# Two attention layers in one kernel: one set of theta and phi copies, reciprocals a slot sooner

## The chip, the core and the metric

The kernel runs on one core of a Trainium2 chip (trn2). The time is the device time of one execution of the whole program in microseconds, and the median over several executions counts. The core has a matrix engine (TensorE, PE in the profile; its weight loads are PEld), a vector engine (VectorE, DVE), a scalar engine (ScalarE, ACT), GpSimd (POOL) and SyncE (SP). SP computes nothing here: it issues every DMA, one after the other in a fixed order, and a wait in its program holds back all that stands behind it.

## What is computed

32 images of 128 channels by 1024 pixels pass through a non-local block and then an attention block with group norm. All inputs and outputs are float32.

```python
# layer 0, d = 64; t and p are (n, 64, 1024), g is x as (n, 128, 1024)
theta = W_theta x + b_theta;  phi = W_phi x + b_phi
f = softmax(einsum('ndq,ndk->nqk', t, p) / sqrt(64), axis=-1)
x1 = x + W_fuse einsum('nqk,nck->ncq', f, g) + b_fuse
# layer 1, c = 128
h = group_norm(x1, 32 groups, eps=1e-5) * gn_w + gn_b
q, k, v = W_q h + b_q, W_k h + b_k, W_v h + b_v
attn = softmax(einsum('bic,bcj->bij', q, k) / sqrt(128), axis=-1)
y = x1 + W_p einsum('bcj,bij->bci', v, attn) + b_p
```

## The kernel before

**Rounds and slots.** The program is a software pipeline. Each round has 16 slots. In slots 0 to 7 PE makes the scores of the eight 128-query tiles of layer 0 of one image, in slots 8 to 15 those of layer 1 of the image before it, each tile 128 x 1024 in PSUM (`s_ps`, three parts). Every engine has a `body` that goes through the 16 slots and calls its steps; the order of these calls is the order of its instructions. `before(what, it, s)` only counts how often something has happened, to give a semaphore's value. A round takes some 57 us. I write round 992 for the one whose first scores start at 991.83 us of the span, round 934 for 934.24, and round 1049 for 1048.64.

**A tile's way.** PE makes the scores; DVE takes the negated row maximum (L750); ACT takes the exponential (L649) and its float16 part (L674), DVE the rest (L767). Both parts lie in `pair`, and a DMA transpose (L364, issued by SP) turns them into `et`. I call the transpose of the tile of slot t "T" and t. Four tiles are a group. Its last tile (slots 3, 7, 11, 15) is turned by PE instead, and DVE finishes it with L761. Its first one (0, 4, 8, 12) is "copied": its rest is made by POOL (L892, `pair<-e_copied,pair`) in the slots of `LO_SLOTS`, and SP issues its transpose in the slot after that.

**Values.** Six slots after a group's first tile, PE begins its products with the values (`values`, `o_ps<-et,v_hi`), for which all transposes of the group must have landed. So the group of slots 12 to 15 is waited for in slot 2 of the next round, the group of slots 0 to 3 in slot 6.

**Reciprocals.** The row sums `den` of a group become factors on DVE (L779, L784) six slots after its first tile, in slots 6, 10, 14 and 2. SP writes them to DRAM (L378) in the same slot and reads them back onto all partitions (L389) in the slot after; the second of these waits on SP until the first has landed. DVE uses them in `normalised` (L804), ten slots after the group's first tile.

**Theta and phi.** In units `tp0` (slot 10) and `tp1` (slot 12) PE makes theta and phi of the next image, 512 pixels each. ACT stages them (L616), and POOL splits each in the next slot into a high and a low part in `tp_hl0` and `tp_hl1`, theta on partitions 0 to 63, phi on 64 to 127 (L889, L892). Four SBUF-to-SBUF DMAs of each half (L424 to L427) then fill `phi2` and `theta2`, in slot 12 and in slot 14. PE's first scores of a round wait for all eight (L463 to L465).

Of the kernel before, what the change touches and what calls it, by code (L numbers as in the profile page):

```python
# [7 lines left out]
F32 = mybir.dt.float32  # L8
# [6 lines left out]
C = 128  # L15
D = 64
# [7 lines left out]
PV_LAG = 6  # L24
OUT_LAG = 10
Y_LAG = 2

# [3 lines left out]
COPIED = 0  # L31
LO_SLOTS = {0: 2, 4: 7, 8: 10, 12: 14}

PART = (0, 1, 0, 2, 1, 0, 1, 2) * 2
# [23 lines left out]
XS_SLOT = 1  # L58
X_MAX_SLOT = 7
X_SLOT = 8  # L60
X_LO_SLOTS = (9, 11)
H_SLOT = 2
H_LO_SLOTS = (3, 4)
RES_SLOTS = (5, 12)
TP_COPY_SLOTS = {12: "tp0", 14: "tp1"}
TP_COPIES = 4
# [10 lines left out]
def attention_pair(nc: bass.Bass, x, w_theta_t, w_phi_t, w_fuse_t, q_w_t, k_w_t, p_w_t, v_w, vectors,  # L77
# [69 lines left out]
    def before(what, it, s):  # L147

        return value(lambda i: count(what, i, s), it)

    def here(what, it, s):
        return bool(what(SLOTS * it.like + s))
# [48 lines left out]
    with ExitStack() as ctx:  # L201
        def sb(name, shape, dt=F32):
            return ctx.enter_context(nc.sbuf_tensor(name, shape, dt))
# [4 lines left out]
        def sem(name):  # L208
            return ctx.enter_context(nc.semaphore(name))
# [25 lines left out]

        tp_hl = [sb(f"tp_hl{n}", [C, 2, HALF], F32R) for n in range(2)]
        q_hi, q_lo = sb("q_hi", [C, N], F32R), sb("q_lo", [C, N], F32R)
# [74 lines left out]
        s_den = sem("den_scaled_ready")  # L312
        s_tp_copy = [sem(f"theta_phi_copied{n}") for n in range(2)]
        s_split_hi = sem("unit_split_hi")
# [24 lines left out]
        def _(sp):  # L339
# [9 lines left out]
            def transposes(it, s):  # L349
                if here(crossed_at, it, s - 2):  # L350
                    move(it, s - 2, crossed_at, s_pair)
                for t in [t for t in LO_SLOTS if LO_SLOTS[t] == s - 1]:
                    move(it, t, copied_at, s_copied)
# [14 lines left out]
            def reciprocals_out(it, s):  # L368
                first = s - 6
                if not (first % GROUP == 0 and here(tile_at, it, first)):  # L370
                    return
                n, g = before(group_at, it, first), first // GROUP % 2
                sp.wait_ge(s_rden, n + 1)
                sp.sem_inc(s_carrier)

                sp.wait_ge(s_rden_row[g], 16 * before(same_group(first), it, first))
                sp.sem_inc(s_carrier)
                sp.dma_start(rden_dram[g], rden[:, g, :]).then_inc(s_rden_dram[g], 16)  # L378

            def reciprocals_in(it, s):  # L380
                first = s - 7
                if not (first % GROUP == 0 and here(tile_at, it, first)):
                    return
                n, g = before(group_at, it, first), first // GROUP % 2
                sp.wait_ge(s_rden_dram[g], 16 * before(same_group(first), it, first) + 16)
                sp.sem_inc(s_carrier)
                sp.wait_ge(s_taken, or_none(n - 1))
                sp.sem_inc(s_carrier)
                sp.dma_start(rden_row[:, g, :],  # L389
                             rden_dram[g].rearrange("q t -> (q t)").partition_broadcast(P)).then_inc(s_rden_row[g], 16)  # L390
# [21 lines left out]
            def tp_copies(it, s):  # L412
                unit = next((u for u, name in UNITS.items() if name == TP_COPY_SLOTS.get(s)), None)
                if unit is None or not here(tp_at, it, unit):
                    return
                half = int(UNITS[unit][-1])
                cols = slice(half * HALF, (half + 1) * HALF)
                sp.wait_ge(s_split, before(staged_at, it, unit) + 1)
                sp.sem_inc(s_carrier)

                sp.wait_ge(s_scores, before(tile_at, it, PHASE))
                sp.sem_inc(s_carrier)
                theta_hl, phi_hl = (tp_hl[half][rows, :, :].bitcast(F32) for rows in (slice(0, D), slice(D, C)))
                sp.dma_start(phi2[0:D, :, cols].bitcast(F32), phi_hl).then_inc(s_tp_copy[half], 16)  # L424
                sp.dma_start(phi2[D:C, :, cols].bitcast(F32), phi_hl).then_inc(s_tp_copy[half], 16)  # L425
                sp.dma_start(theta2[0:D, cols].bitcast(F32), theta_hl[:, 0, :]).then_inc(s_tp_copy[half], 16)  # L426
                sp.dma_start(theta2[D:C, cols].bitcast(F32), theta_hl[:, 1, :]).then_inc(s_tp_copy[half], 16)  # L427

# [14 lines left out]
        def _(pe):  # L443
# [7 lines left out]
            def scores(it, s, half):  # L451
                if not here(tile_at, it, s):
                    return
                if half == 0:
# [8 lines left out]
                    if s == 0:  # L463
                        for n in range(2):
                            pe.wait_ge(s_tp_copy[n], 16 * TP_COPIES * before(mx_at, it, 0))  # L465
                    if s == PHASE:
# [233 lines left out]
        def _(dve):  # L700
# [70 lines left out]
            def reciprocals(it, s):  # L771
                first = s - 6
                if not (first % GROUP == 0 and here(tile_at, it, first)):
# [104 lines left out]
        def _(pool):  # L878
# [15 lines left out]
            def split_units(it, s):  # L894
# [7 lines left out]
                if name[0] == "t":  # L902

                    pool.wait_ge(s_tp_copy[half], 16 * TP_COPIES * or_none(before(mx_at, it, s) - 1))
                    hi, lo = tp_hl[half][:, 0, :], tp_hl[half][:, 1, :]
                    hi_read = hi.bitcast(F32)
# [150 lines left out]
```

## Time and profile before

| | us |
|---|---|
| median of 3 runs | 1922.38 (1917.98 to 1924.8) |
| the profiled execution | 1909.72 |
| its span in the trace | 1907.9 |
| PE busy in it | 1715.2 (90%) |
| POOL, ACT, DVE busy | 1381.1, 1409.7, 1359.3 |

The profile is one execution, 0.66% below the median of the runs. Its times are from the start of the span. The chain that ended last is made up of PE to 44%, of SP's queue to 20%, of "issue" to 12% and of DMAs to 8%. The issuing time of a DMA on SP and the time until it lands are two things: a row of SP's queue shows the first, and the page lists medians of the second: 3.8 us for the theta copies, 4.6 us for the transposes, 2.1 us for the reciprocals' write. The page's DMA share is the mean over 16 engines.

### The profile page before, as it was taken

Reading aid. Unit: us, or ns where it says so; the run is one execution under the profiler, and the core shown is the slowest. Engines: PE = TensorE matmul, PEld = TensorE weight load, DVE = VectorE, ACT = ScalarE, POOL = GpSimd, SP = SyncE. Lnnn points to the kernel's source line nnn. Section 1 sums busy time; section 2 is a strip of 40 time slices with the busy share of each in tenths; the row PEclk is TensorE's granted clock in tenths of the full one; section 3 lists DMA queues with packets and bytes.
Section 4 is the critical chain, followed back from the end, with each engine's and each line's share of the span. In section 5 each row is a group of like instructions: output and inputs, shape, how many; then the busy total and the mean of one; then the engine's idle time right before and its main releaser. Section 6 shows DMA issues by size and latency. Waiting matters only on the chain.

```text
span 1907.9 us, 34651 instructions
## 1 busy us (share of the span) xinstructions
PE 1715.2 (90%) x8970; PEld 1127.0 (59%) x8970; DVE 1359.3 (71%) x1541; ACT 1409.7 (74%) x2088; POOL 1381.1 (72%) x1449
## 2 busy tenths in 40 slices
PE   4698989999999999999989999999999999999986
PEld 3465655665656665665655655665656666655653
DVE  4577777777777777777777777777777777777764
ACT  3577777778777777877777877777877777877764
POOL 3567776778777778777778777678777778877754
PEclk9999999999999999999999999999999999999999
DMA  4688888888888888888887878888878988878874
GB/s 94 127 160 169 165 174 166 182 178 171 171 176 180 178 181 167 170 170 177 180 182 166 172 169 181 174 175 172 173 170 172 187 180 168 170 168 184 167 145 94
DMA packets 879542, 319.90 MB, mean 168 GB/s; under 512 B 825376, under 2 KB 826272, under 8 KB 879520
## 3 DMA queue, kind: packets, MB, share of 16 engines
q1 hardware_dynamic: 879520, 319.65, 81.3%
q8 instruction: 9, 0.15, 0.0%
q14 instruction: 13, 0.11, 0.0%
HBM read 50.86 MB, written 17.04 MB: 36 GB/s over the span
## 4 chain that ended last, share of the span: by engine, by line
PE 44%; SPq 20%; issue 12%; DMA 8%; POOL 5%; ACT 5%; DVE 4%; POOLq 0%; ACTq 0%; DVEq 0%
PE o_ps L448 17%; PE s_ps L448 16%; SPq L364 10%; PE m_ps L448 6%; DMA theta<-tp_hl 6%; PE s_ps L487 5%; SPq L426 2%; SPq L424 2%; SPq L427 2%; SPq L425 2%; DVE neg_max L750 2%; DMA rden_dram<-rden 1%; POOL k_lo L892 1%; DVE pair L767 1%; ACT e L649 1%
## 5 line engine op out<-in xcount | busy, mean ns | idle before, releaser
L750 DVE TENSOR_REDUCE neg_max<-s_ps 128x1 f32<-128x1024 f32 x512 | 625.5, 1222 | 233.3 <-PE s_ps L448 232.7
L448 PE MATMUL o_ps<-et,v_hi 128*128 128x512 f16 x2048 | 702.7, 385 | 57.5 <-issue 31.2
L448 PE MATMUL s_ps<-phi,theta 128*128 128x512 f32 x1024 | 334.5, 450 | 95.2 <-DMA theta<-tp_hl 86.2
L448 PE MATMUL o_ps<-et,v_lo 128*128 128x512 f16 x1024 | 393.4, 384 | 0.0
L448 PEld LDWEIGHTS o_ps<-et,v_hi 128*128 128x128 f16 x2048 | 204.8, 100 | 303.0 <-issue 98.2
L767 DVE SCALAR_TENSOR_TENSOR pair<-s_ps,pair 128x1024 f16<-128x1024 f32 x256 | 311.2, 1216 | 16.8 <-ACT pair L674 16.8
L649 ACT ACTIVATE s_ps<-s_ps,neg_max 128x1024 f32<-128x1024 f32 x256 | 277.3, 1083 | 58.9 <-DVE neg_max L750 58.3
L448 PEld LDWEIGHTS s_ps<-phi,theta 128*128 128x128 f32 x1024 | 197.2, 196 | 167.6 <-issue 102.4
L892 POOL TENSOR_TENSOR pair<-e_copied,pair 128x1024 f16<-128x1024 f32 x128 | 273.8, 2139 | 22.5 <-ACT pair L672 22.5
L761 DVE SCALAR_TENSOR_TENSOR et<-s_ps,et 128x1024 f16<-128x1024 f32 x128 | 156.8, 1225 | 175.4 <-ACT et L659 175.4
L674 ACT ACTIVATE pair<-s_ps 128x1024 f16<-128x1024 f32 x256 | 261.9, 1023 | 17.5
L448 PE MATMUL s_ps<-k_hi,q_hi 128*128 128x512 f32 x512 | 249.4, 487 | 4.4 <-POOL q_lo L892 2.1
L448 PE MATMUL s_ps<-k_hi,q_lo 128*128 128x512 f32 x512 | 202.0, 395 | 0.0
L448 PE MATMUL s_ps<-k_lo,q_hi 128*128 128x512 f32 x512 | 200.5, 392 | 0.0
L649 ACT ACTIVATE e<-s_ps,neg_max 128x1024 f32<-128x1024 f32 x128 | 142.6, 1114 | 52.5 <-DVE neg_max L750 52.4
L659 ACT ACTIVATE et<-s_ps 128x1024 f16<-128x1024 f32 x128 | 131.1, 1024 | 62.5 <-PE s_ps L487 55.7
L986 POOL TENSOR_TENSOR x<-x,xr 128x512 f32<-128x512 f32 x64 | 81.6, 1275 | 110.1 <-DVE x L804 110.0
L487 PE MATMUL s_ps<-ident_sb,e 128*128 128x128 f32 x1024 | 147.8, 292 | 10.4 <-ACT e L649 10.3
L892 POOL TENSOR_TENSOR v_lo<-stage,v_hi 128x512 f16<-128x512 f32 x128 | 148.2, 1157 | 10.7
L487 PEld LDWEIGHTS s_ps<-ident_sb,e 128*128 128x128 f32 x1024 | 129.2, 153 | 34.8 <-ACT e L649 23.3
L649 ACT ACTIVATE e_copied<-s_ps,neg_shifted 128x1024 f32<-128x1024 f32 x128 | 142.9, 1116 | 4.1
L448 PEld LDWEIGHTS o_ps<-et,v_lo 128*128 128x128 f16 x1024 | 101.8, 99 | 69.4 <-issue 3.3
(130 smaller groups left out, 2873.0 us busy)
## 6 DMA issues: line engine op xcount, KB each, us to landing
phi<-tp_hl SPq DMA_DIRECT2D x128, 256.0 KB, 3.8
rden_row<-rden_dram SPq DMA_DIRECT2D x128, 256.0 KB, 3.8
xs<-in_x SPq DMA_DIRECT2D x32, 512.0 KB, 4.0
theta<-tp_hl SPq DMA_DIRECT2D x128, 128.0 KB, 3.8
out_y<-y_sb SPq DMA_DIRECT2D x64, 256.0 KB, 2.4
et<-pair SPq DMA_TRANSPOSE x384, 4.6
rden_dram<-rden SPq DMA_DIRECT2D x128, 2.0 KB, 2.1
w_f<-in_w_fuse_t SPq DMA_DIRECT2D x1, 64.0 KB, 2.3
```

The lines of the kernel that those rows point to most:

```text
L364: sp.dma_start_transpose(et[:, t // GROUP % 4, r, :, :], pair[:, place(t), :, :].rearrange("q a n -> q (a n)")).then_inc(s_pair_t[place(t) ...
L424: sp.dma_start(phi2[0:D, :, cols].bitcast(F32), phi_hl).then_inc(s_tp_copy[half], 16)
L448: mm = pe.matmul(out, lhs_t, rhs, start=start and n == 0, stop=stop and n == len(terms) - 1)
L487: mm = pe.transpose(s_ps[:, part(t), kb * P:(kb + 1) * P], e[:, kb * P:(kb + 1) * P], ident[:, :])
L649: nc.scalar.activation(to[:, :], s_ps[:, r, :], ACT.Exp, bias=bias, accum_out=den[:, g, t % GROUP:t % GROUP + 1]).then_inc(s_exp, 1)
L659: nc.scalar.activation(et[:, t // GROUP % 4, TURNED, 0:KB, :], s_ps[:, part(t), :].rearrange("k (b q) -> k b q", b=KB), ACT.Copy, scale=E_ ...
L674: nc.scalar.activation(pair[:, r, 0, :], s_ps[:, part(t), :], ACT.Copy, scale=E_SCALE).then_inc(s_pair_hi, 1)
L750: nc.vector.tensor_reduce(neg_max[:, t % 4:t % 4 + 1], s_ps[:, part(t), :], AX.X, ALU.max, negate=True).then_inc(s_max, 1)
L761: nc.vector.scalar_tensor_tensor(out=blocks[:, KB:2 * KB, :], in0=s_ps[:, part(t), :].rearrange("k (b q) -> k b q", b=KB), scalar=E_SCALE, ...
L767: nc.vector.scalar_tensor_tensor(out=pair[:, r, 1, :], in0=s_ps[:, part(t), :], scalar=E_SCALE, in1=pair[:, r, 0, :], op0=ALU.mult, op1=AL ...
L892: nc.gpsimd.tensor_tensor(out, in_, hi, ALU.subtract).then_inc(sem, 1)
L986: nc.gpsimd.tensor_tensor(x1[:, cols], x1[:, cols], xr[:, cols], ALU.add).then_inc(s_x1, 1)
```

## The change

It does three things.

- **One set of copies.** `tp_hl0` and `tp_hl1` become one tile `tp_hl` of 1024 columns. SP issues four DMAs of twice the size, all in slot 13, after it has waited for the split of `tp1`. They replace four in slot 12 and four in slot 14; the diff shows one of the four. One semaphore replaces two.
- **Reciprocals a slot sooner.** With `REC_LAG = 5` DVE makes them in slots 5, 9, 13 and 1; SP writes them in the same slots and reads them back in slots 6, 10, 14 and 2. In slot 13 the write stands ahead of the copies, in slot 1 ahead of the image load.
- **The last copied tile first.** T12 is issued in slot 14, ahead of T13, and no longer in slot 15 behind it.

```diff
+REC_LAG = 5
+COPIED_OUT_SLOTS = {0: 3, 4: 8, 8: 11, 12: 14}
-TP_COPY_SLOTS = {12: "tp0", 14: "tp1"}
+TP_COPY_SLOT = 13
...
-        tp_hl = [sb(f"tp_hl{n}", [C, 2, HALF], F32R) for n in range(2)]
+        tp_hl = sb("tp_hl", [C, 2, N], F32R)
...
             def transposes(it, s):
                 if here(crossed_at, it, s - 2):
                     move(it, s - 2, crossed_at, s_pair)
-                for t in [t for t in LO_SLOTS if LO_SLOTS[t] == s - 1]:
+                for t in [t for t in COPIED_OUT_SLOTS if COPIED_OUT_SLOTS[t] == s]:
                     move(it, t, copied_at, s_copied)
...
             def reciprocals_out(it, s):
-                first = s - 6
+                first = s - REC_LAG
...
             def reciprocals_in(it, s):
-                first = s - 7
+                first = s - REC_LAG - 1
...
             def tp_copies(it, s):
-                unit = next((u for u, name in UNITS.items() if name == TP_COPY_SLOTS.get(s)), None)
-                if unit is None or not here(tp_at, it, unit):
-                    return
-                half = int(UNITS[unit][-1])
-                cols = slice(half * HALF, (half + 1) * HALF)
-                sp.wait_ge(s_split, before(staged_at, it, unit) + 1)
+                if s != TP_COPY_SLOT or not here(mx_at, it, MX_SLOT):
+                    return
+                sp.wait_ge(s_split, before(staged_at, it, s))
...
-                sp.dma_start(phi2[0:D, :, cols].bitcast(F32), phi_hl).then_inc(s_tp_copy[half], 16)
+                sp.dma_start(phi2[0:D, :, :].bitcast(F32), phi_hl).then_inc(s_tp_copy, 16)
...
             def reciprocals(it, s):
-                first = s - 6
+                first = s - REC_LAG
```

On SP, in the repeated round, from slot 11 on. Before (L364 are the transposes, here T9, T8, T10, then T13 and T12 behind the copies):

```order
L364 DMA_TRANSPOSE et<-pair 128x16x128
L418 ISA
L421 ISA
L424 DMA phi2<-tp_hl0 64x2x512
L425 DMA phi2<-tp_hl0 64x2x512
L426 DMA theta2<-tp_hl0 64x512
L427 DMA theta2<-tp_hl0 64x512
L376 ISA
L378 DMA rden_dram<-rden 128x4
L418 REGISTER_ALU
L424 DMA phi2<-tp_hl1 64x2x512
L425 DMA phi2<-tp_hl1 64x2x512
```

The same place after the change (the line numbers are four to five higher):

```order
L368 DMA_TRANSPOSE et<-pair 128x16x128
L380 ISA
L382 DMA rden_dram<-rden 128x4
L419 ISA
L422 ISA
L425 DMA phi2<-tp_hl 64x2048
L426 DMA phi2<-tp_hl 64x2048
L427 DMA theta2<-tp_hl 64x1024
L428 DMA theta2<-tp_hl 64x1024
L389 REGISTER_ALU
L393 DMA rden_row<-rden_dram 128x512
```

The reciprocals' write moved from between the two sets to ahead of the single one; eight copies became four.

On DVE, around slot 1, before and after as one piece of the difference. The first row is the last operation on the turned tile of slot 15:

```order
 L761 SCALAR_TENSOR_TENSOR et<-s_ps,et 128x1024
+L779 SCALAR_TENSOR_TENSOR den_scaled<-den,v_scale1,e_factors 128x4
+L783 ISA
+L784 RECIPROCAL rden<-den_scaled 128x4
 L749 REGISTER_ALU
 L750 TENSOR_REDUCE neg_max<-s_ps 128x1
 L793 REGISTER_ALU
-L794 ISA
-L804 TENSOR_TENSOR y_sb<-o_ps,rden_row 128x512
-L779 SCALAR_TENSOR_TENSOR den_scaled<-den,v_scale1,e_factors 128x4
-L784 RECIPROCAL rden<-den_scaled 128x4
```

The two small operations moved ahead of a row maximum and of `normalised`.

## Rows read from the trace of the kernel before

**Rows 1.** The page: busy time and its share of the span, by engine.
```profile
PE 1715.2 (90%) x8970; PEld 1127.0 (59%) x8970; DVE 1359.3 (71%) x1541; ACT 1409.7 (74%) x2088; POOL 1381.1 (72%) x1449
```

**Rows 2.** Waits of PE: total us, times, longest; other waits left out.
```profile
PE s_ps L448 <- DMA theta<-tp_hl: 86.2, 31, 5.0
PE o_ps L448 <- issue: 31.2, 33, 2.4
PE o_ps L448 <- POOL k_lo L892: 15.2, 12, 1.5
...
PE o_ps L448 <- DMA et<-pair: 11.0, 6, 3.6
```

**Rows 3.** PE in time: start, us, line; brackets: idle before, releaser.
```profile
991.83 1.17 PE L448 MATMUL s_ps<-phi,theta 128*128 128x512 f32 x4 [2.50 <-DMA theta<-tp_hl]
...
1013.88 0.38 PE L448 MATMUL o_ps<-et,v_hi 128*128 128x512 f16 x1 [1.13 <-POOL k_lo L892]
```

**Rows 4.** The chain that ended last, in the round starting at 934.24: start, us.
```profile
942.28 4.12 DMA rden_dram<-rden
...
947.25 2.97 SPq L364
...
952.69 4.52 DMA et<-pair
```

**Rows 5.** SP's queue in time: transposes, copies, reciprocals (start, us of issuing).
```profile
973.51 7.82 SPq L364 DMA_TRANSPOSE et<-pair  x3
981.68 0.67 SPq L424 DMA_DIRECT2D phi<-tp_hl  x1
...
985.47 0.37 SPq L378 DMA_DIRECT2D rden_dram<-rden  x1
986.10 0.62 SPq L424 DMA_DIRECT2D phi<-tp_hl  x1
...
988.13 1.29 SPq L427 DMA_DIRECT2D theta<-tp_hl  x1
...
990.31 7.76 SPq L364 DMA_TRANSPOSE et<-pair  x3
...
1003.51 7.82 SPq L364 DMA_TRANSPOSE et<-pair  x3
...
1060.28 8.73 SPq L364 DMA_TRANSPOSE et<-pair  x3
```

**Rows 6.** Stretches of the copies: busy by engine, PEclk, DMA share, GB/s.
```profile
984.00:986.00 2.00, 2.00 (x17) 1.58 (x16) 1.97 (x3) 1.47 (x2) 2.00 (x2) 1.00 0.97 188
986.50:987.50 1.00, 1.00 (x6) 0.83 (x5) 0.81 (x2) 0.97 (x3) 1.00 (x2) 1.00 0.39 76
990.00:991.50 1.50, 0.00 (x0) 0.00 (x0) 0.42 (x1) 0.61 (x2) 0.00 (x0) 1.00 0.79 250
```

**Rows 7.** DVE and POOL in time: start, us, instruction.
```profile
979.77 1.23 DVE L761 SCALAR_TENSOR_TENSOR et<-s_ps,et 128x1024 f16<-128x1024 f32 x1 [1.40 <-ACT et L659]
980.16 1.29 POOL L892 TENSOR_TENSOR tp_hl<-stage,tp_hl 128x512 fp32r<-128x512 f32 x1
...
998.90 0.22 DVE L779 SCALAR_TENSOR_TENSOR den_scaled<-den,v_scale,e_factors 128x4 f32<-128x4 f32 x1
...
1000.39 1.21 DVE L767 SCALAR_TENSOR_TENSOR pair<-s_ps,pair 128x1024 f16<-128x1024 f32 x1
...
1058.80 1.21 DVE L767 SCALAR_TENSOR_TENSOR pair<-s_ps,pair 128x1024 f16<-128x1024 f32 x1
```

**Rows 8.** Stretches: two rounds' first parts, then two round starts.
```profile
991.83:1013.88 22.05, 20.00 (x105) 12.95 (x106) 15.61 (x17) 18.36 (x28) 15.80 (x20) 1.00 0.90 195
1048.64:1071.15 22.51, 21.68 (x105) 14.25 (x106) 15.24 (x17) 17.77 (x27) 15.23 (x20) 0.92 0.95 193
...
130.70:132.70 2.00, 2.00 (x9) 1.71 (x9) 0.79 (x1) 0.17 (x1) 0.24 (x2) 0.50 1.25 170
1792.70:1794.70 2.00, 2.00 (x10) 1.76 (x9) 0.95 (x1) 0.17 (x1) 0.41 (x3) 0.53 1.17 201
```

More of the change, by code:

```diff
@@ L312, in attention_pair @@
         s_den = sem("den_scaled_ready")
-        s_tp_copy = [sem(f"theta_phi_copied{n}") for n in range(2)]
+        s_tp_copy = sem("theta_phi_copied")
         s_split_hi = sem("unit_split_hi")
@@ L422, in tp_copies @@
                 sp.sem_inc(s_carrier)
-                theta_hl, phi_hl = (tp_hl[half][rows, :, :].bitcast(F32) for rows in (slice(0, D), slice(D, C)))
-                sp.dma_start(phi2[0:D, :, cols].bitcast(F32), phi_hl).then_inc(s_tp_copy[half], 16)
-                sp.dma_start(phi2[D:C, :, cols].bitcast(F32), phi_hl).then_inc(s_tp_copy[half], 16)
-                sp.dma_start(theta2[0:D, cols].bitcast(F32), theta_hl[:, 0, :]).then_inc(s_tp_copy[half], 16)
-                sp.dma_start(theta2[D:C, cols].bitcast(F32), theta_hl[:, 1, :]).then_inc(s_tp_copy[half], 16)
+                theta_hl, phi_hl = (tp_hl[rows, :, :].bitcast(F32) for rows in (slice(0, D), slice(D, C)))
+                sp.dma_start(phi2[0:D, :, :].bitcast(F32), phi_hl).then_inc(s_tp_copy, 16)
+                sp.dma_start(phi2[D:C, :, :].bitcast(F32), phi_hl).then_inc(s_tp_copy, 16)
+                sp.dma_start(theta2[0:D, :].bitcast(F32), theta_hl[:, 0, :]).then_inc(s_tp_copy, 16)
+                sp.dma_start(theta2[D:C, :].bitcast(F32), theta_hl[:, 1, :]).then_inc(s_tp_copy, 16)
             def body(it):
@@ L463, in scores @@
                     if s == 0:
-                        for n in range(2):
-                            pe.wait_ge(s_tp_copy[n], 16 * TP_COPIES * before(mx_at, it, 0))
+                        pe.wait_ge(s_tp_copy, 16 * TP_COPIES * before(mx_at, it, 0))
                     if s == PHASE:
@@ L902, in split_units @@
                 if name[0] == "t":
-                    pool.wait_ge(s_tp_copy[half], 16 * TP_COPIES * or_none(before(mx_at, it, s) - 1))
-                    hi, lo = tp_hl[half][:, 0, :], tp_hl[half][:, 1, :]
+                    pool.wait_ge(s_tp_copy, 16 * TP_COPIES * or_none(before(mx_at, it, s) - 1))
+                    hi, lo = (tp_hl[:, n, half * HALF:(half + 1) * HALF] for n in range(2))
                     hi_read = hi.bitcast(F32)
```

1 line of the change is left out of this document (added).

## The prediction

> **What bounds the kernel now.** I read the busy shares first, then PE's waits, then one round in time on PE and on SP, then the stretches in which DMAs move.
>
> PE is busy for 90% of the span; no other engine is over 74% [rows 1]. So PE is the bound, and what can be won is its waits. Two kinds make up most of them [rows 2]. Before the first scores of a round PE waits for the theta copies: 86.2 us in 31 rounds, 2.8 each. Before products with the values it waits 31.2 + 15.2 + 11.0 = 57.4 us under three names. The names mislead. In round 934 the chain goes from the landing of the reciprocals' write (942.28 + 4.12 = 946.40) over T1 at 947.25 to T2 at 952.69, which lands at 957.21 and lets PE's products go [rows 4]. So there the wait is for the last transpose of the group, also where the waits name POOL or "issue"; and T1 stood behind the reciprocals on SP.
>
> In round 992 the three waits are 2.50 us before the first scores [rows 3], and between these and the products of slot 6 22.05 - 20.00 = 2.05 us of idle PE [rows 8]: 1.13 in slot 6 [rows 3], the other 0.92 in slot 2, where T14 is the last transpose to be waited for. Two kinds of rounds must be kept apart. In round 992 PE's granted clock is 1.00 throughout (2.4 GHz). In round 1049 it is 0.92 over the same part, PE is busy for 21.68 us with the same 105 matmuls and idle for 0.83 [rows 8]: after the wait for theta it starts at half speed (1.2 GHz). Of the 30 rounds from 130 to 1792 us, 17 start so, the first and the last among them [rows 8], and 13 at full speed. In a half-speed round the slow start uses up what would otherwise be waited.
>
> **Part 1, one set of copies.** Now: T10 is issued by 973.51 + 7.82 = 981.33, the first copy at 981.68, the second set at 986.10, its last at 988.13 [rows 5], and PE starts at 991.83 [rows 3], 10.15 after the first copy. PE could have started 2.50 sooner. Afterwards the first copy waits for three things: T10 (981.33), the split of tp1 (980.16 + 1.29 = 981.45), and the new reciprocals' write ahead of it. The latter needs DVE's L761 (979.77 + 1.23 = 981.00 [rows 7]) and two small operations of some 0.2 us (0.22 for the larger one [rows 7]), so about 981.5. The three come within 0.2 us of each other. The write with what follows it takes 986.10 - 985.47 = 0.63 [rows 5]. The first copy goes out at about 982.35, 0.65 later than now.
>
> Against it stands a hole that goes away. Between the two sets DMA is mostly idle: 986.5 to 987.5 moves at a share of 0.39, so 0.6 us are lost [rows 6]. 0.65 and 0.6 cancel. What is left is the moving itself. The copies of a round are 4 x 256 + 4 x 128 KB = 1.57 MB. With 2.1 us (the time to land of the small reciprocals' write) as the fixed part, they take 10.15 - 2.1 - 0.6 = 7.45 us, 211 GB/s; the DMA engines are busy to 0.97 at 188 GB/s in the middle and 0.79 at 250 at the end [rows 6]. This is a transfer at its limit, and halving the number of DMAs halves neither bytes nor time. Bounds: at 250 GB/s 6.3 us, 1.15 us sooner; at 188 GB/s all the way 8.4 us, 0.95 later. I take 0.2 us sooner, near the middle rate since the same bytes take the same way, a little for fewer and longer rows: 30 x 0.2 = 6 us.
>
> The Trainium skill says otherwise twice (DMA: Bandwidth & Descriptors). "Rules for kernel authors" asks for large transfers, and the fit in "Anatomy of one DMA" (2.0 us and bytes over 436 GB/s, for another issuing path) would give 5.6 us for all 1.57 MB, an estimate. "Why small descriptors are slow (HBM only)" says that SBUF-to-SBUF transfers don't suffer from small ones, which would leave nothing to win. The trace agrees with the second: 188 GB/s at a share of 0.97. By the first the wait for theta would be gone (below, with rival B).
>
> Once there is a loss. At the start of the pipeline tp1's split comes long after tp0's, and nothing but the spacing of the two sets bounds what is lost: 986.10 - 981.68 = 4.4 us at most [rows 5]. I take 3 us.
>
> **Part 2, reciprocals sooner and T12 first.** In round 992 the half of T1 in `pair` is ready at 1000.39 + 1.21 = 1001.60 [rows 7], but SP issues it at 1003.51 [rows 5], since it stands in the wait for the reciprocals' write, whose turn came late and which queued behind transposes and the image load. DVE's two operations begin at 998.90 now; a slot sooner they stand two large operations earlier, of some 1.2 us each [rows 7]. So the write is issued some 2.4 us sooner, ahead of the image load, and the read is out of the way by about 1001. T1 then goes at 1001.8, 1.7 sooner, and T0 and T2 with it, each ready by then. Against this, DVE's two operations now stand ahead of the row maximum of slot 2: 0.45 us, of which its later slack takes half, so 0.25. Net 1.45, and PE's products of slot 6 come at 22.05 - 1.45 = 20.6 after the first scores instead of 22.05. For this the wait in slot 2 (0.92) must shrink too, or 20.00 + 0.92 = 20.9 would be the end. It does in part: with four DMAs less and T12 ahead, SP begins the last three transposes at some 987.5 and not at 990.31 [rows 5]. But DMA is taken by the copies until about 991, so T14 lands only some 0.5 sooner. 20.4 is then under 20.6. For the 13 full-speed rounds I take 1.5: 20 us.
>
> In a half-speed round this gives little. In round 1049 T1 is issued at 1060.28 [rows 5] with its pair ready at 1058.80 + 1.21 = 1060.01 [rows 7]: SP was not late, and at most the 0.83 us of idle PE could go. Other such rounds had T1 held back by a few tenths. Bounds 0 and 0.83; I take 0.4: 17 x 0.4 = 7 us.
>
> The other places to which reciprocals move cost nothing: the writes of slots 5 and 9 fall where SP waits for the next pair anyway (T9 at 973.51 began a new batch). In slot 13 DVE's 0.45 us fall into a wait for PE of about that length. `rden_row` is needed five slots after it is read. If such cover were gone, it would be 0.4 us for each group.
>
> **Sum.** 6 + 20 + 7 - 3 = 30 us. The profiled execution would go from 1909.7 to about 1880; the median of the runs is 0.66% above it now, so from 1922.4 to 1892, 1.6% faster. With the bounds of part 2 and rates near the middle this case runs from 1878 to 1908.
>
> **Rivals.**
>
> A, the gain is only partial: SP is free in time, but something else holds the slot 6 products (T0 or T2 late, or the wait in slot 2 unchanged at 0.92). Then 13 x 0.5 + 6 - 3 = 10 us: 1912. For it: T14 depends on a DMA that is full. Against: the three rows from T1 to T2 follow each other without a gap.
>
> B, the large copies are quicker, and the clock holds. For it: 250 GB/s is seen at the end of the set [rows 6]. Copies 1.15 us sooner leave 1.35 of the 2.50 us wait; a shorter wait might leave the clock at its upper level, and a half-speed round would be like a full one (22.51 to 20.6, 1.5 more than the 0.4 counted). 30 x 1.15 + 17 x 1.5 + 24 = 84 us: 1838. By the Trainium skill's fit named above (DMA: Bandwidth & Descriptors, "Anatomy of one DMA") the wait for theta would end altogether, and the time would be about 1795, an estimate. Against both: the share of 0.97.
>
> C, slower: issuing and landing grow with the size of a DMA, so that merging wins nothing and the set no longer starts early. Now the last copy is issued 2.03 us after the first of its set, and PE goes on 3.70 after that. If both grew by 40%, PE would start at 982.35 + 2.8 + 5.2 = 990.3, sooner than now; doubled, at 982.35 + 4.1 + 7.4 = 993.8, 2.0 us later. The case decides against the change from 24 / 30 = 0.8 us later on, since part 2 gives 24 us. At 1.4 us later: 42 - 24 = 18 us slower, 1940. For it: the gate now has three things that end together, and each delay hits all the bytes. Against: the first set's rate shows that its issues weren't the limit.
>
> D, nothing: what is won before slot 6 is waited for again at the next theta copies, or half-speed starts become more frequent (13 full rounds that turn half-speed lose what they won). 1920.
>
> **Chances.** Forecast 0.50, A 0.10, B 0.17, C 0.12, D 0.11. A measurement of this kernel can tell about 0.3% (6 us) from no change. Faster by more than that: 0.50 + 0.10 + 0.17, and a little of D, 0.78; within it 0.10; slower 0.12. The range takes in the forecast, A, about half of B and most of D: 1840 to 1922. The likeliest time is 1892.
>
> **What the profile will show.** If part 1 is right, PE's wait for theta stays near 2.3 us a round (75 us in all or a little less), with the last copy landing some 10 us after T10's issue, and no hole in the DMA share. If part 2 is right, T1 follows its pair by 0.3 us in all rounds, SP's wait for the reciprocals' write (L386 before) shrinks to under half, and the waits before products fall from 57 to some 25 us. The count of half-speed round starts tells the clock's part. A wait for theta under 1.5 us is B, one over 3.3 us is C. The forecast is wrong if the copies' rate changes by over 10%, or if the number of half-speed starts moves by more than five.

## The result, and the profile after

The changed kernel takes 1907.78 us (median of 5 runs, 1903.28 to 1910.44) beside 1922.38 us before (5 runs, 1917.98 to 1924.8). The ratio is 0.9927, with a 95% interval of 0.9906 to 0.9948: 0.7% or 14.6 us faster, where 30 us were forecast. In a second measurement, beside other runs of the kernel before, the same kernel gave 0.9973 (0.9955 to 0.9991). Both intervals lie below 1, so the gain is real, but it is 0.3 to 0.7%. The larger figure rests on the first measurement alone: there the kernel before took 1922 us, in three later groups 1908 to 1910, and why is not known.

The two profiled executions don't even show it: 1909.72 us before and 1910.44 after. That of before lay 12.7 us under the median of its runs, that of after 2.7 over. The kernel before took such a time in the later groups too. The two still show well what moved, and on what its size depends.

First the page: busy time by engine, then the engines' shares of the chain of work that ended last.

```profile
PE 1738.8 (91%) x8970; PEld 1141.4 (60%) x8970; DVE 1383.4 (72%) x1541; ACT 1404.0 (74%) x2088; POOL 1379.7 (72%) x1449
...
PE 42%; issue 14%; DMA 11%; POOL 11%; ACT 9%; SPq 6%; DVE 4%; POOLq 0%; ACTq 0%; DVEq 0%
```

PE does the same 8970 matmuls as before and is busy for 23.6 us longer [rows 1]. DVE has its 1541 instructions again, and is busy for 24.1 us longer. Both matter below. PE's waits (total us, times, longest):

```profile
PE s_ps L449 <- DMA theta<-tp_hl: 99.7, 31, 8.7
...
PE o_ps L449 <- issue: 10.8, 11, 2.7
...
PE o_ps L449 <- DMA et<-pair: 5.1, 2, 3.3
...
PE o_ps L449 <- DVE y_sb L804: 3.3, 6, 1.2
```

Before products PE waits 20.1 us under all names (k_lo's 0.9 with them), where it was 57.4 [rows 2]: 37 us less. For theta it waits 99.7 instead of 86.2: 13.5 more. All in all its waits are 23 us shorter, and its busy time 23.6 us longer. The busy time is the clock's: stretches of 2 us, each from 0.5 us after a round's first scores on (busy by engine PE, PEld, DVE, ACT, POOL, then the granted clock, DMA share and GB/s):

```profile
1053.60:1055.60 2.00, 2.00 (x15) 1.63 (x15) 1.23 (x1) 0.32 (x2) 0.71 (x3) 1.00 1.14 219
1109.64:1111.64 2.00, 2.00 (x9) 1.71 (x8) 0.60 (x1) 0.17 (x1) 0.13 (x1) 0.50 1.07 219
```

Of the 30 rounds behind the start-up, 5 start at full clock like the first row, 25 wholly or partly at half like the second; before it was 13 and 17 [rows 8]. I sorted the rounds by the clock of this stretch, and took the mean time from one round's first scores to the next's:

| | rounds, full clock | their mean, us | rounds, mostly at half | their mean, us | third round begins at |
|---|---|---|---|---|---|
| before | 13 | 57.07 | 10 | 57.51 | 130.2 |
| after | 5 | 56.26 | 17 | 57.45 | 135.4 |
| after, second measurement | 9 | 56.22 | 13 | 57.26 | 137.0 |

(The rest have a clock between 0.6 and 0.98 in it, and the last has no successor.) So full-speed rounds became 0.8 us shorter, half-speed rounds did not, and full-speed rounds became rare. The second measurement's profiled execution had 9 of them and a span 9 us shorter. That goes with the lower median of the changed kernel there, 1901.79 us instead of 1907.78. Why its lead was nevertheless smaller it doesn't explain: that comes from the kernel before, which took 1909.95 us instead of 1922.38.

### The profile page after: what moved, and what is told of

Same layout as the page of the kernel before. It is cut to its first block, busy times and chain, and to the rows that moved or that the text cites. A ratio compares the mean times of both kernels' runs of the same rounds, so it can differ in the third digit from the quotient of the medians.

```text
span 1908.6 us, 34400 instructions
## 1 busy us (share of the span) xinstructions
PE 1738.8 (91%) x8970; PEld 1141.4 (60%) x8970; DVE 1383.4 (72%) x1541; ACT 1404.0 (74%) x2088; POOL 1379.7 (72%) x1449
## 4 chain that ended last, share of the span: by engine, by line
PE 42%; issue 14%; DMA 11%; POOL 11%; ACT 9%; SPq 6%; DVE 4%; POOLq 0%; ACTq 0%; DVEq 0%
PE o_ps L449 15%; PE s_ps L449 15%; DMA theta<-tp_hl 10%; PE m_ps L449 6%; PE s_ps L487 6%; SPq L427 3%; ACT s_ps L649 3%; POOL x_lo L892 2%; ACT et L659 2%; DVE den_scaled L779 2%; ACT h_hi L628 2%; ACT e L649 2%; DVE neg_max L750 1%; POOL tp_hl L892 1%; POOL y_sb L996 1%
## 5 line engine op out<-in xcount | busy, mean ns | idle before, releaser
L449 PE MATMUL o_ps<-et,v_hi 128*128 128x512 f16 x2048 | 709.9, 388 | 20.5 <-issue 10.8
L449 PE MATMUL s_ps<-phi,theta 128*128 128x512 f32 x1024 | 343.3, 460 | 108.9 <-DMA theta<-tp_hl 99.7
L449 PEld LDWEIGHTS s_ps<-phi,theta 128*128 128x128 f32 x1024 | 201.8, 201 | 184.1 <-DMA theta<-tp_hl 102.6
L892 POOL TENSOR_TENSOR pair<-e_copied,pair 128x1024 f16<-128x1024 f32 x128 | 274.2, 2142 | 22.2 <-ACT pair L672 22.2
L761 DVE SCALAR_TENSOR_TENSOR et<-s_ps,et 128x1024 f16<-128x1024 f32 x128 | 156.8, 1225 | 180.0 <-ACT et L659 180.0
L674 ACT ACTIVATE pair<-s_ps 128x1024 f16<-128x1024 f32 x256 | 262.2, 1024 | 17.6
L659 ACT ACTIVATE et<-s_ps 128x1024 f16<-128x1024 f32 x128 | 131.1, 1024 | 71.8 <-PE s_ps L487 65.4
L487 PE MATMUL s_ps<-ident_sb,e 128*128 128x128 f32 x1024 | 155.0, 301 | 12.1 <-ACT e L649 12.1
L487 PEld LDWEIGHTS s_ps<-ident_sb,e 128*128 128x128 f32 x1024 | 135.5, 159 | 37.9 <-ACT e L649 27.0
L892 POOL TENSOR_TENSOR v_lo<-stage,v_hi 128x512 f16<-128x512 f32 x128 | 148.2, 1158 | 10.7
L672 ACT ACTIVATE pair<-e_copied 128x1024 f16<-128x1024 f32 x128 | 135.3, 1057 | 9.2
```

The lines of the kernel that those rows point to most:

```text
L449: mm = pe.matmul(out, lhs_t, rhs, start=start and n == 0, stop=stop and n == len(terms) - 1)
L487: mm = pe.transpose(s_ps[:, part(t), kb * P:(kb + 1) * P], e[:, kb * P:(kb + 1) * P], ident[:, :])
L659: nc.scalar.activation(et[:, t // GROUP % 4, TURNED, 0:KB, :], s_ps[:, part(t), :].rearrange("k (b q) -> k b q", b=KB), ACT.Copy, scale=E_ ...
L672: nc.scalar.activation(pair[:, r, 0, :], e_copied[:, :], ACT.Copy).then_inc(s_copied_hi, 1)
L674: nc.scalar.activation(pair[:, r, 0, :], s_ps[:, part(t), :], ACT.Copy, scale=E_SCALE).then_inc(s_pair_hi, 1)
L761: nc.vector.scalar_tensor_tensor(out=blocks[:, KB:2 * KB, :], in0=s_ps[:, part(t), :].rearrange("k (b q) -> k b q", b=KB), scalar=E_SCALE, ...
```

## What stands ahead of the copies

This is one round of the changed kernel in time: DVE, then POOL, SP and PE (start, us, instruction; in brackets the idle time before and what ended it).

```profile
1040.14 1.23 DVE L761 SCALAR_TENSOR_TENSOR et<-s_ps,et 128x1024 f16<-128x1024 f32 x1 [1.40 <-ACT et L659]
1041.28 1.13 DVE L779 SCALAR_TENSOR_TENSOR den_scaled<-den,v_scale,e_factors 128x4 f32<-128x4 f32 x1
1042.54 0.18 DVE L784 RECIPROCAL rden<-den_scaled 128x4 f32<-128x4 f32 x1
```

```profile
1041.11 1.29 POOL L892 TENSOR_TENSOR tp_hl<-stage,tp_hl 128x512 fp32r<-128x512 f32 x1
```

```profile
1033.65 7.08 SPq L368 DMA_TRANSPOSE et<-pair  x3
1042.98 0.33 SPq L382 DMA_DIRECT2D rden_dram<-rden  x1
1043.65 0.51 SPq L425 DMA_DIRECT2D phi<-tp_hl  x1
...
1046.77 2.50 SPq L428 DMA_DIRECT2D theta<-tp_hl  x1
1049.53 1.08 SPq L393 DMA_DIRECT2D rden_row<-rden_dram  x1
1050.86 8.55 SPq L368 DMA_TRANSPOSE et<-pair  x3
```

```profile
1053.10 1.19 PE L449 MATMUL s_ps<-phi,theta 128*128 128x512 f32 x4 [3.37 <-DMA theta<-tp_hl]
1062.14 0.39 PE L449 MATMUL o_ps<-et,v_hi 128*128 128x512 f16 x1 [0.94 <-issue]
1074.53 0.38 PE L449 MATMUL o_ps<-et,v_hi 128*128 128x512 f16 x1 [0.45 <-DVE y_sb L804]
```

Three things are to be seen.

- **SP stands idle for over 2 us.** T9, T8 and T10 are out at 1033.65 + 7.08 = 1040.73, not 7.82 but 7.08 after they began [rows 5]. The first copy leaves at 1043.65. T10 is no gate any more; all the copies wait for the split of the last half and for the reciprocals' write.
- **A 4-column operation takes 1.13 us.** The sums' scaling, L779, takes 0.21 alone. Here it overlaps POOL's L892, which runs till 1042.39, and ends at 1042.41, 0.02 behind it. The write follows, and behind it the copies. Over the whole execution the scaling takes over 0.3 us in 71 of 128 cases, before in 25, and each of the 71 ends within 0.03 us behind the end of an instruction of POOL; together it takes 74.9 us instead of 49.4, which is all the growth of DVE's busy time. In 14 of the 30 rounds the first copy left some 1.25 us after the split, in 14 others 0.24, in two between.
- **The issues grew.** From the first copy to the last it is 3.12 us where a set took 2.03 before, and PE starts 6.33 after the last, where it was 3.70.

The Trainium skill has the second point (SBUF — State Buffer, "Who interferes with whom"): a DVE instruction with two inputs from SBUF contends with a GpSimd instruction that reads SBUF, and whichever engine has the shared pair keeps it for a whole instruction. The trace agrees: 1.13 us instead of 0.21, and the end 0.02 us behind POOL's. The reciprocal behind it, with one input, took 0.18 in all 128 cases, also in the 57 that lay inside an instruction of POOL with two inputs.

## Experiments

The kernels ran in three groups of four, each with the kernel before beside it, at 1908.15, 1908.53 and 1909.95 us. That is 0.7% under the 1922.38 of the first measurement, so ratios are compared, not times. The same changed kernel gave 0.9927 in one group and 0.9973 in another, so between groups a difference of half a per cent tells nothing.

### The reciprocals alone

```diff
 (kernel before)
+REC_LAG = 5
-                first = s - 6
+                first = s - REC_LAG
...
-                first = s - 7
+                first = s - REC_LAG - 1
```

> Only the reciprocals move a slot sooner; two sets of copies in slots 12 and 14 as before. My theory (the single set starts too late, since it waits for the split of tp1 and for a reciprocals' write that POOL holds up): the waits before products fall as they did after the change (from 57 to about 20 us), and the first set of copies can start right behind T10, which is now issued sooner; the wait for theta falls from 86 to about 60 us. Time 1855 to 1885, clearly below the changed kernel's 1908. The rival (merging the copies is good, and what went wrong is only that more rounds start at half speed): no better than the changed kernel, 1903 to 1915.

Measured: 1973.86 us, ratio 1.0352 (1.0323 to 1.0380), 3.5% slower. Both expectations were wrong. SP in one round says why:

```profile
1071.00 0.68 SPq L425 DMA_DIRECT2D phi<-tp_hl  x1
...
1073.23 1.28 SPq L428 DMA_DIRECT2D theta<-tp_hl  x1
1074.79 0.36 SPq L379 DMA_DIRECT2D rden_dram<-rden  x1
1077.20 0.33 SPq L390 DMA_DIRECT2D rden_row<-rden_dram  x1
1077.78 0.62 SPq L425 DMA_DIRECT2D phi<-tp_hl  x1
```

The write now stands in slot 13, and the read in slot 14 ahead of the second set of copies. SP issues in order, and the read must wait until the write has landed: from 1075.15 to 1077.20 it stands still, with half of theta and phi behind it. PE waits 155.5 us for theta in all, and all 30 rounds start at half clock. The benefit that I had counted on is there too, product waits of 10.7 us; it is worth little beside this.

### Reciprocals and T12, without the merging

```diff
 (the kernel above)
+COPIED_OUT_SLOTS = {0: 3, 4: 8, 8: 11, 12: 14}
-                for t in [t for t in LO_SLOTS if LO_SLOTS[t] == s - 1]:
+                for t in [t for t in COPIED_OUT_SLOTS if COPIED_OUT_SLOTS[t] == s]:
```

> The changed kernel with the merging alone undone: reciprocals sooner, T12 first, two sets of copies in slots 12 and 14. My theory: as with the reciprocals alone within 5 us, since T12 first only changes which of three transposes goes first; 1855 to 1885. The rival: 1903 to 1915, as changed.

Measured: 2049.58 us, 1.0735 (1.0712 to 1.0758). Now a transpose stands ahead of the second set as well; PE waits 240.3 us for theta. Both expectations were wrong again. So this isn't "the change without its merging", as I had meant: with sets in slots 12 and 14, part 2 is harmful.

### The merging alone

```diff
 (changed kernel)
-REC_LAG = 5
+REC_LAG = 6
-COPIED_OUT_SLOTS = {0: 3, 4: 8, 8: 11, 12: 14}
+COPIED_OUT_SLOTS = {0: 3, 4: 8, 8: 11, 12: 15}
```

> Only the copies are merged in slot 13; reciprocals and T12 as before. The write of the reciprocals then stands behind the set and lands behind it, and the three last transposes wait for its landing. My theory: the waits before products stay at 57 us or grow (slot 2), the wait for theta is near 2.5 us a round; 1915 to 1940. The rival: the wait for theta is shorter than before and the time is 1895 to 1912.

Measured: 1979.28 us, 1.0359 (1.0326 to 1.0391), outside both expected ranges. My theory had the direction and the place, the write's landing ahead of the last transposes, far too small. PE waits 79.0 us for theta, 20.7 less than after the change, but 91.8 before products. SP after the copies:

```profile
1080.76 2.49 SPq L428 DMA_DIRECT2D theta<-tp_hl  x1
1083.51 1.18 SPq L382 DMA_DIRECT2D rden_dram<-rden  x1
1087.37 0.33 SPq L393 DMA_DIRECT2D rden_row<-rden_dram  x1
1087.94 3.01 SPq L368 DMA_TRANSPOSE et<-pair  x1
```

Nothing stands between write and read any more. SP waits 2.7 us between them, with T13 behind; over the execution its waits for the write's landing are 251.2 us, where the changed kernel has 93.0.

The three runs give one rule: something long has to stand on SP between the reciprocals' write and their read. Before it was the second set [rows 5], after it is the single one. The reciprocals alone and the merging alone each take it away and cost over 3%. That is why the prediction's sum, part by part, could not be checked part by part.

### The sums' scaling without its second input

```diff
 (changed kernel)
-                nc.vector.scalar_tensor_tensor(out=den_scaled[:, :], in0=den[:, g, :], scalar=v_scale[layer][:, 0:1],
-                                               in1=e_factors[:, :], op0=ALU.mult, op1=ALU.mult).then_inc(s_den, 1)
+                nc.vector.tensor_scalar(den_scaled[:, 0:1], den[:, g, 0:1], v_scale[layer][:, 0:1], 1.0, ...
+                nc.vector.tensor_scalar(den_scaled[:, 1:GROUP], den[:, g, 1:GROUP], v_scale[layer][:, 0:1], E_SCALE, ...
```

> The changed kernel, with the first of DVE's two small operations (den_scaled, with two inputs in SBUF) made as two operations with one SBUF input each. In the trace of the changed kernel it ends some 20 ns after a running POOL operation in 78 of 128 cases and takes up to 1.3 us instead of 0.2. My theory: it no longer waits for POOL, so in about half the rounds the set of copies starts 1.0 us sooner, the waits for theta are all near 2.65 us, and the time falls by 10 to 15 us, to about 1895. The rival (this is coincidence, something else holds DVE): no change, 1908.

Measured: 1928.26 us, 1.0118 (1.0087 to 1.0148). This made it worse, which neither theory nor rival had. The 3-column operation was held up in its turn (in one round it took 1.27 us and ended 0.02 us behind POOL's), now in nearly all rounds, so that the first copy left 1.26 us behind the split in them, and the wait for theta rose to 115.3 us. So the second input isn't all that decides. The Trainium skill names this too (SBUF — State Buffer, "Who interferes with whom"): `tensor_scalar` can enter a mode that uses both of DVE's ports, and then contends like the other. No trace shows the mode itself. What they show agrees in so far as the operation of 3 columns was held up (over 0.3 us in 80 of 128 cases), and one of 1 column never took over 0.21 us (512 cases, next run). With four operations of one column:

```diff
 (changed kernel, in place of the scalar_tensor_tensor)
+                for t in range(GROUP):
+                    nc.vector.tensor_scalar(den_scaled[:, t:t + 1], den[:, g, t:t + 1], v_scale[layer][:, 0:1],
+                                            E_SCALE if t else 1.0, ALU.mult, ALU.mult).then_inc(s_den, 1)
+                dve.wait_ge(s_den, GROUP * n + GROUP)
```

> The changed kernel with the sums' scaling (one operation of 4 columns with two inputs from SBUF on DVE) written as four operations of one column with one input. Theory (the 4-column operation is held up by whatever POOL runs, up to 1.1 us, and with it the reciprocals' write that stands ahead of the copies on SP): no operation is held up, the first copy leaves 0.25 us behind POOL's split in all rounds, theta waits 2.7 in all of them, about 30 x 0.4 = 12 us less than the changed kernel. Rival (DVE has no room for three more operations at that place, or its hold-up moves to the next one): level with the changed kernel or slower by up to 10 us.

Measured: 1905.33 us, 0.9983 (0.9971 to 0.9994). The hold-up is gone; DVE and POOL at the place:

```profile
1037.21 0.57 DVE L780 TENSOR_SCALAR den_scaled<-den,v_scale 128x1 f32<-128x1 f32 x4
```

```profile
1037.23 1.28 POOL L893 TENSOR_TENSOR tp_hl<-stage,tp_hl 128x512 fp32r<-128x512 f32 x1
```

Four operations take 0.57 us right beside POOL's. But nothing is gained, as the rival said: the first copy leaves 9.7 us behind the end of T9's pair on DVE in nearly all rounds, where the changed kernel has 9.2 in 14 of them and 9.4 to 10.2 in the other 16. The time without the hold-up is about the mean of what it was with it, presumably since four small operations, the reciprocal and the write still have to come one after another between DVE's L761 and the copies. The hold-up is real, and it isn't what decides the change.

### Two sets, each as soon as its half is split

```diff
 (changed kernel)
-TP_COPY_SLOT = 13
+TP_COPY_SLOTS = {12: "tp0", 13: "tp1"}
...
-                if s != TP_COPY_SLOT or not here(mx_at, it, MX_SLOT):
+                unit = next((u for u, name in UNITS.items() if name == TP_COPY_SLOTS.get(s)), None)
+                if unit is None or not here(tp_at, it, unit):
...
-                sp.dma_start(phi2[0:D, :, :].bitcast(F32), phi_hl).then_inc(s_tp_copy, 16)
+                sp.dma_start(phi2[0:D, :, cols].bitcast(F32), phi_hl).then_inc(s_tp_copy[half], 16)
```

> The changed kernel, but theta and phi copied again in two sets of four transfers (half 0 in slot 12, half 1 in slot 13), reciprocals and the fourth group's tile as changed. It is the kernel with the merging alone undone, and it keeps the second set ahead of the reciprocals' read and of the fourth group's tile on SP. Theory (the one large set lands late because it can leave only after POOL has ended half 1's split, while half 0's could have gone 3 us earlier): theta wait per round under 1.5 us where the changed kernel has 2.7 to 3.5, product waits stay near 20 us in all, 3 to 5% faster than before. Rival (what costs is the landing of the last copies, the same with two sets, and the reciprocals' write stands between the sets and delays the second): theta wait 2.7 or more as before the change, time level with the changed kernel, or above it by what the second wait on SP costs.

Measured: 1841.82 us, ratio 0.9665 (0.9638 to 0.9692): 3.4% faster than before. SP and PE in one round:

```profile
1047.58 7.01 SPq L368 DMA_TRANSPOSE et<-pair  x3
1054.93 0.81 SPq L428 DMA_DIRECT2D phi<-tp_hl  x1
...
1058.78 0.37 SPq L382 DMA_DIRECT2D rden_dram<-rden  x1
1059.40 0.62 SPq L428 DMA_DIRECT2D phi<-tp_hl  x1
...
1061.45 1.29 SPq L431 DMA_DIRECT2D theta<-tp_hl  x1
1063.00 0.37 SPq L393 DMA_DIRECT2D rden_row<-rden_dram  x1
1063.62 7.87 SPq L368 DMA_TRANSPOSE et<-pair  x3
```

```profile
1065.24 1.16 PE L452 MATMUL s_ps<-phi,theta 128*128 128x512 f32 x4 [1.53 <-DMA theta<-tp_hl]
```

The scaling was held up in this kernel too (0.87 us in this round), but half 0's copies leave right behind T10 (1047.58 + 7.01 = 1054.59), and the reciprocals are made beside them. The second set is sent 0.6 us behind the write, and the read waits for nothing, since 3.3 us of copies stand ahead of it. From the end of T9's pair on DVE to the first scores it takes 17.75 us on the mean of 30 rounds; before 18.77, after the change 19.14. SP's waits for `rden` are 23.9 us, where the changed kernel has 79.3. The theory was right, if a little high: the wait is 1.6 us a round and not under 1.5, and the gain is at the lower end of its 3 to 5%. PE's waits, and a round's start:

```profile
PE s_ps L452 <- DMA theta<-tp_hl: 52.2, 31, 5.0
PE o_ps L452 <- issue: 36.7, 43, 2.6
```

```profile
1065.74:1067.74 2.00, 2.00 (x16) 1.62 (x15) 1.22 (x1) 0.35 (x2) 0.74 (x3) 1.00 1.18 229
```

29 of 30 rounds start at full clock. PE waits 52 us for theta and is busy for 1688.7, 50 us less than after the change. Product waits are 51.7, higher than the 20 expected. They come with full-speed rounds: the changed kernel with all its rounds at full clock ("The clock", below) has 43.2, with copies and reciprocals as in the changed kernel, which has 20.1.

### The kernel before with its second set a slot sooner

```diff
 (kernel before)
-TP_COPY_SLOTS = {12: "tp0", 14: "tp1"}
+TP_COPY_SLOTS = {12: "tp0", 13: "tp1"}
```

> The kernel before with one number changed: the second set of copies in slot 13 instead of slot 14, which puts it ahead of the reciprocals' write on SP; reciprocals, tile 12 and buffers as before. Theory (what pays in the kernel with two sets is only that each set leaves as soon as its half is split): theta wait under 1.5 us a round, 2 to 4% faster than before, level with the two sets kernel within 1%. Rival (the earlier reciprocals are needed too, since their write and read, a slot later, now land behind the copies and the first group's product waits for its reciprocals or SP waits for the write in front of tile 13): theta wait falls, but SP waits for the write's landing rise above 200 us and product waits to 80 us or more, 0 to 3% slower than before.

Measured: 1977.55 us, 1.0340 (1.0300 to 1.0381). The rival was right, and sharper than it said. The wait for theta falls to 62.6 us, 20 rounds start at full clock, and yet it is 3.4% slower: write and read are neighbours again, SP waits 228.4 us for landings, and PE 106 before products. The first name on PE's list:

```profile
PE o_ps L448 <- DMA et<-pair: 77.4, 30, 4.8
```

So the early reciprocals are needed with early copies, and the other way round. With the two together, two sets give 3.4%, and as much with T12 as before (0.9642, below).

### The clock

```diff
 (changed kernel, on PE ahead of the wait for the copies)
+FILL = 8
+                        pe.wait_ge(s_evac, before(taken_at, it, s))
+                        for _ in range(FILL):
+                            pe.matmul(m_ps[:, :], w_hl["tp"][:, 0, :], x_hi[:, 0:HALF], start=True, stop=True)
```

> The changed kernel with eight matmuls more on PE ahead of the wait for theta, on tiles that are there and into a bank that is free; they compute nothing that is used, and are to keep TensorE's clock up while it waits. Theory (25 of 30 rounds start at half clock because PE stands still for 2.7 to 3.5 us, where before the change 17 did; half speed costs 1 to 2 us a round): the half-clock starts go, 20 to 30 us less than the changed kernel. Rival (the work after the start is set by other engines, so half speed there costs nothing): level, or slower by what of the eight matmuls (1.7 us at full clock) outlasts the wait.

Measured: 1882.44 us, 0.9867 (0.9848 to 0.9886). One place of it:

```profile
1090.39 2.19 PE L468 MATMUL m_ps<-x_hi,w_tp_hl 128*128 128x512 f32 x8
1093.69 1.19 PE L450 MATMUL s_ps<-phi,theta 128*128 128x512 f32 x4 [1.10 <-DMA theta<-tp_hl]
```

```profile
1094.19:1096.19 2.00, 2.00 (x16) 1.64 (x15) 1.23 (x1) 0.32 (x2) 0.71 (x3) 1.00 1.07 218
```

The copies are no sooner: 19.29 us from T9's pair to the first scores. But all 30 rounds start at full clock, and a round takes 56.13 us on the mean, the 56.26 of the changed kernel's five full-speed rounds. The changed kernel's mean over all its rounds is 57.14. 29 x 1.0 = 29 us, and the two profiled spans differ by 1908.6 - 1878.7 = 29.9. So its half-speed starts cost the changed kernel about 1 us a round. By the ratios, for which the changed kernel was measured in other groups, it is 0.6 to 1.1%, 11 to 20 us; the theory was right about the starts, and its 20 to 30 us hold between the profiles only. How much of it is due to the idle stretch being shorter (1.1 us) rather than to PE's work in it, this run doesn't tell.

The price of a half-speed start isn't a constant either. In the kernel before it was 57.51 - 57.07 = 0.44 us. Where PE waits long before products, none is to be seen: in the kernel before with its second set a slot sooner, 20 rounds that start at full clock take 59.91 us on the mean, and 7 that start at half take 58.55.

### The fourth group's tile, and combinations

> The changed kernel with the fourth group's copied tile issued in slot 15 again, behind the three turned ones: the third part of the change alone undone. Theory (product waits of slot 2 fell because this tile lands first; putting it back brings some back, but nothing moves ahead of the copies): product waits rise by 5 to 20 us in all, theta waits unchanged, 0 to 15 us slower than the changed kernel. Rival (this part did nothing, or it delays the first group's tiles): within 3 us, or faster.

```diff
 (changed kernel; and likewise the one with two sets)
-COPIED_OUT_SLOTS = {0: 3, 4: 8, 8: 11, 12: 14}
+COPIED_OUT_SLOTS = {0: 3, 4: 8, 8: 11, 12: 15}
```

Measured: 1902.29 us, 0.9965 (0.9950 to 0.9980). Product waits came out at 14.3 us, not above 20.1 but under it. The rival was right: this part does nothing that can be told. With two sets the same:

> The two sets kernel with the fourth group's copied tile back in slot 15, behind the turned ones. Theory (as with the merged set, this part moves a product wait or two of under 1 us a round): within 0.5% of two sets. Rival (with PE no longer waiting 2.7 us and more for theta, the products of slot 2 are what PE waits for next, and this tile was the last of them): 0.5 to 2% slower than two sets.

Measured: 1839.58 us, 0.9642 (0.9617 to 0.9667), level with two sets.

> The two sets kernel with the sums' scaling as four operations of one column. Theory (with two sets the write stands between them, and half 0's issues, 3 us, cover its hold-up by POOL): level with two sets within 0.3%. Rival (the reciprocals still come late in some rounds, SP waits for rden 24 us in 36 waits there): 0.5 to 1% faster than two sets.

Measured: 1837.20 us, 0.9616 (0.9587 to 0.9645), the best of all, 3.8% faster than before. The interval overlaps with that of two sets, which ran in another group, and the profiled spans are 1838.7 and 1838.0 us; nothing shows that the four small operations bring anything here.

> The changed kernel once more, on the chip of the three that follow, for comparison. First theory (the merged set, late, is what keeps the change small): 0.99 to 0.996 of the time before, as in the first measurement. Rival (the changed kernel's lead is a matter of the chip): 1.0 within 0.3%.

Measured: 1901.79 us, 0.9973 (0.9955 to 0.9991), told above. The first theory's range is missed, the rival's holds: in this measurement the lead is just inside the 0.3% that I took as told from no change, though its interval stops short of 1. So the differences among the changed kernel, the one with four small operations and the one with T12 back (0.9927 and 0.9973, 0.9983, 0.9965) are not told apart.

## Why the prediction was off

The forecast was 1892 us; it is 1907.78. The direction was right. That the range held it says little, since 1840 to 1922 reaches from 4% faster to no change. The mechanisms were mostly the right ones, but three terms of the sum were mis-sized: the loss before the first copy, what part 2 gives to a round, and the number of half-speed starts, put at no change.

The profiled rounds show how much each did. The 29 intervals between first scores were 57.31 us on the mean before, 57.07 for the 13 full-speed rounds and 57.50 for the others; they are 57.14 now, 56.26 for 5 and 57.32 for 24. With 13 and 16 rounds as before, that is 13 x 0.81 + 16 x 0.18 = 13.4 us, where the forecast had 6 + 20 + 7 = 33. The eight rounds that turned half-speed take back 8 x (57.32 - 56.26) = 8.5, the start 5.2. Nothing is left, and the two profiled spans are equal within 0.7 us.

By its own steps:

- **Part 1, the copying itself: right.** From first copy to first scores it was 10.2 us on the mean of 30 rounds, and is 9.5, 0.65 sooner; the hole and the rate were put at 0.8. Rival C's sizes came true within it (issues 54% longer, landing 71%), and still the set as a whole was quicker, since only the last one counts.
- **Part 1, when the first copy leaves: this step failed.** It said three gates within 0.2 us and a loss of 0.65. T10 was out 1.2 to 3.1 us ahead of the first copy. The "two small operations of some 0.2 us" took 1.4 us together in the round shown (1041.28 to 1042.72), and the first copy was late by it in about half of the rounds. Behind the end of T9's pair it leaves 9.61 us on the mean of 30 rounds, before 8.58: 1.03 later, not 0.65. In the rounds without the hold-up it is 9.16, 0.58 later, so the rest of the step was right. A row of DVE that takes 0.22 [rows 7] was taken as its price anywhere, though the place it moved to lies beside POOL's split; 25 cases of over 0.3 us were in the trace of before. From T9's pair to the first scores a round takes 0.4 us longer than before, not 0.2 less: 30 x 0.6 = 18 us off. Behind it lay a question that was not asked: I weighed one set against two sets in slots 12 and 14, and not against what SP and the DMAs could do in the time in which the single set waits. The run with two sets shows 1.4 us a round there.
- **Part 1, start-up: too small.** The third round begins 5.2 us later than before, not 3.
- **Part 2, SP is free in time: right.** T1 is issued at 1063.21, 0.23 us behind its pair's end at 1062.98, as foretold; SP's waits for the write's landing fell from 153.8 to 93.0 us, above the half that was named. Product waits are 20.1 us, forecast 25.
- **Part 2, 1.5 us for a full-speed round: this step failed too.** From the first scores to the products of slot 6 full-speed rounds took 22.4 us on the mean and take 21.4, 1.0 less instead of 1.45; whole rounds became 0.8 shorter, where with the copies 1.7 had been forecast. In the round shown the products start at 1074.53 - 1053.10 = 21.43 after the first scores, 22.05 before, 20.6 forecast. The wait in slot 2 was to shrink and is still 0.94. Sum: 20.04 busy + 0.94 + 0.45 for `y_sb`. That is rival A in this place, for the reason it names. In this round T14 lands 8.8 us after the first scores as before, though T12 leaves 0.7 us sooner. It was to leave 2.8 sooner; but issuing the four large copies took until 1046.77 + 2.50 = 1049.27, 5.6 us in all, and the read behind them 1.08.
- **Part 2, 0.4 us for a half-speed round: nothing.** 57.51 became 57.45. In the 17 rounds that started below full clock T1 had been issued 0.2 to 2.0 us behind its pair, not "a few tenths", and is now issued 0.23 behind it in nearly all of them: there T1 was not what held the round.
- **The number of half-speed starts: rival D, 8.5 us.** It was taken as fixed at 17 and went to 25, 21 in the second measurement's profile. A full-speed round of the changed kernel that turns half-speed loses 57.45 - 56.26 = 1.2 us, more than the 0.8 by which full-speed rounds became shorter. "Moves by more than five" was named as what would make the forecast wrong. D had a chance of 0.11, and the reason why starts should become more frequent, a longer wait for theta, was not tied to the question of when the first copy leaves; they were one question.

The prediction's sum also took the parts as separate. The runs show that they aren't: the reciprocals alone are 3.5% slower, the merging alone 3.6%. T12 alone was not run; taken out of the changed kernel and of the one with two sets it made no difference.

## What to carry to other kernels

On an engine that issues in order, a write and the read that waits for it need something long between them, which doesn't wait itself; before moving one of the two, or what stands between, list the queue as it will be. Merging transfers makes all of their bytes wait for the last producer: count what the queue could do in that time, since here two sets, sent as each half was ready, beat one by some 3% (0.9665 against 0.9927 and 0.9973). And count a wait of PE twice, once for itself and once for the clock at which the work behind it starts; the second was worth 1 us a round here, where PE had little else to wait for, and less where it had.

## What the runs showed of the hardware

- **DVE beside POOL.** A 4-column operation took 1.13 us instead of 0.21, to 0.02 us behind the end of POOL's instruction. A 3-column `tensor_scalar` with one input was held up in the same way (1.27 us); one-column ones (0.20 to 0.21 us each, overlapping, 0.57 for four) and the 4-column reciprocal (0.18) were not. All 71 cases over 0.3 us in the changed kernel ended within 0.03 us behind the end of an instruction of POOL, the longest after 1.32 us: what the operation lost went by POOL's instruction, not by its own size.
- **Issuing grows with the transfer.** In the merged set the four issues took 0.51, 0.58, 1.88 and 2.51 us (medians of 32), with half the number of transfers; in the two sets of the round shown 0.81, 0.60, 0.80 and 1.23, then 0.62, 0.61, 0.68 and 1.29. It is the third and the fourth that grow, the first two don't.
- **The clock after a wait.** With waits for theta of 1.3 to 2.1 us, 29 of 30 rounds began at the upper level (2.4 GHz); in the changed kernel, with 2.6 to 4.5 us, 5 of 30 in one execution and 9 in another; with the reciprocals alone, and 4.6 to 6.2 us, none. Waits of the same length were followed by either level in one execution (2.62 by 1.00, 2.63 by 0.50), so the wait alone doesn't set it.
